# A PixArt-style block chain on one core: the cross attention's query pieces, key parts and rows of negated maxima go out by other DMA issues

## The reference, cut to what matters

```
q_c = q_c.reshape(B, N, NH, hd).transpose(0, 2, 1, 3)
k_c = k_c.reshape(B, S, NH, hd).transpose(0, 2, 1, 3)
v_c = v_c.reshape(B, S, NH, hd).transpose(0, 2, 1, 3)
c_attn_w = jax.nn.softmax(jnp.einsum('bhqd,bhsd->bhqs', q_c, k_c) * scale, axis=-1)
c_attn_out = jnp.einsum('bhqs,bhsd->bhqd', c_attn_w, v_c)
```

## Time and profile before

| | |
|---|---|
| median of 3 runs | 5570.83 us (5566.85 to 5578.4) |
| profiled execution, its own time | 5582.41 us |
| its span, first to last instruction | 5580.6 us |
| mean granted TensorE clock over the span | 0.864 of full speed |
| PE busy | 4790.3 us (86%) |
| DVE busy | 3913.3 us (70%) |
| ACT busy | 2961.3 us (53%) |
| POOL busy | 1466.4 us (26%) |
| first exp of the three cross attention phases starts at | 490.7, 2237.8 and 4411.5 us |
| last exp of the three starts at | 1709.0, 3351.5 and 5468.9 us |

### The profile page before, as it was taken

One profiled execution on the slowest core, in us unless ns is written; L12 is line 12 of the kernel. 1 busy time (PEld: TensorE's weight loads), 2 busy tenths in 40 slices (PEclk: granted clock), 3 DMA queues, 4 the chain that ended last, 5 costly groups with the idle time before them and its releaser, 6 DMA issues. The chain is left out here.

```text
span 5580.6 us, 168125 instructions
## 1 busy us (share of the span) xinstructions
PE 4790.3 (86%) x72434; PEld 3025.4 (54%) x72434; DVE 3913.3 (70%) x7814; ACT 2961.3 (53%) x4527; POOL 1466.4 (26%) x1189
## 2 busy tenths in 40 slices
PE   4858999999998585999999997888676799999998
PEld 2634555555554362666666663564364366656654
DVE  5547888888883553888888873465454688889893
ACT  2323666766655332666666663215423366666665
POOL 1013444434420103333333310000200334333320
PEclk6667999999988666999999988999766699999998
DMA  3325555555530334666666630550242565556640
GB/s 81 69 62 174 158 166 172 156 180 159 165 125 10 77 61 140 198 205 206 204 200 201 193 118 18 166 175 1 53 71 54 173 188 188 185 186 193 190 155 17
DMA packets 481664, 766.00 MB, mean 137 GB/s; under 512 B 144922, under 2 KB 381882, under 8 KB 468538
## 3 DMA queue, kind: packets, MB, share of 16 engines
q1 hardware_dynamic: 462394, 741.14, 44.5%
q10 hardware_dynamic: 18528, 14.11, 1.1%
HBM read 465.48 MB, written 287.75 MB: 135 GB/s over the span
## 5 line engine op out<-in xcount | busy, mean ns | idle before, releaser
L1349 DVE TENSOR_REDUCE maxima<-ps 100x1 f32<-100x482 f32 (+1 forms) x4608 | 2743.0, 650 | 580.3 <-PE ps L1169 566.5
L1296 ACT ACTIVATE probs<-ps 128x800 f32<-128x800 f32 (+1 forms) x2304 | 1805.6, 833 | 573.6 <-PE ps L1192 562.7
L1169 PE MATMUL ps<-kst,qst 48*100 48x482 bf16 (+1 forms) x4608 | 1392.6, 420 | 137.1 <-DMA qst<-cross_q_parts 54.9
L1401 POOL TENSOR_TENSOR kparts<-kf,zero 128x512 bf16<-128x512 f32 (+2 forms) x448 | 545.0, 1217 | 2044.2 <-ACT kf L1268 2004.1
L1209 PE MATMUL ps<-probs,vals 128*9 128x100 f32 x36864 | 1047.9, 256 | 1.0 <-ACT probs L1296 0.9
L1209 PEld LDWEIGHTS ps<-probs,vals 128*9 128x9 f32 x36864 | 757.5, 92 | 240.3 <-issue 198.8
L1169 PEld LDWEIGHTS ps<-kst,qst 48*100 48x100 bf16 x4608 | 443.8, 123 | 797.7 <-DVE maxima L1349 452.5
L1192 PE MATMUL ps<-qst,kst 51*128 51x100 bf16 x18432 | 803.8, 210 | 81.2 <-ACT probs L1296 60.6
L1192 PEld LDWEIGHTS ps<-qst,kst 51*128 51x128 bf16 x18432 | 614.4, 99 | 224.9 <-issue 86.4
L763 ACT ACTIVATE probs<-ps 100x800 f32<-100x800 f32 x192 | 159.7, 837 | 369.0 <-PE ps L711 368.6
L1146 PE MATMUL ps<-ctxT,perm_wk_L 128*128 128x512 f32 (+1 forms) x576 | 327.6, 656 | 31.9 <-DMA ctxT<-ctx_turned 17.1
(11 more groups left out here) (260 smaller groups left out, 4528.0 us busy)
## 6 DMA issues: line engine op xcount, KB each, us to landing
kst<-ctx_k_stack SPq DMA_DIRECT2D x96, 2888.0 KB
ctx_k_stack<-kparts SPq DMA_DIRECT2D x192, 541.5 KB
ctx_k_stack<-kparts SPq DMA_DIRECT2D x192, 361.0 KB
ctok<-in_ctx_dram SPq DMA_DIRECT2D x64, 704.0 KB
ctx_k_stack<-kparts SPq DMA_DIRECT2D x192, 180.5 KB
ctx_turned<-ctxT SPq DMA_DIRECT2D x32, 722.0 KB, 3.4
cT<-ctx_turned SPq DMA_DIRECT2D x32, 722.0 KB, 5.5
ctxT<-ctx_turned SPq DMA_DIRECT2D x32, 722.0 KB
```

The source lines that it names most:

```text
L1169: nc.tensor.matmul(ps[0:N, at:at + w], g.qst[s][row0:row0 + CROWS, j, :], g.kst[s][row0:row0 + CROWS, j, a:a + w], start=True, stop=True). ...
L1296: nc.scalar.activation(probs[kt % 2][hf][0:kts[kt], :].rearrange("p (k n) -> p k n", k=2), src, ACT.Exp).then_inc(exp_done, 1)
L1349: nc.vector.reduce_max(maxima[:, col:col + 1], ps[0:N, at:at + widths[c]], AX.X).then_inc(m_read, 1)
L1401: return nc.gpsimd.tensor_tensor(out, src, g.zero[0:src.shape[0], 0:1].to_broadcast(list(src.shape)), ALU.add)
```

## The change

- Query stack: with `SLOT_K` and `SLOT_Q` exchanged, the query parts stand in the slots in the order 0, 1, 2, 0, 1, 0. Neighbouring slots now hold neighbouring rows of the DRAM array, so six DMAs of 24, 16 and 8 rows fill it where twelve of 8 rows did.
- Key parts: the six slots now hold part 0 three times, part 1 twice, part 2 once. Two DMAs write each part, from a source that repeats it, and they wait only for the step of POOL that completed this part (`split`, then `parts_ready`).
- The sums of batch b - 1 are written to DRAM before the context load is issued and read back after it (`sp_out`, `sp_out_back`).
- The six rows of negated maxima are issued by ACT, three after exp 16 and three after exp 17 (`act_negmax`, `plan.turn() + 1` is 8 in all three plans). `sp_negmax` is gone.
- `dve_out` waits for the DMAs that read the same buffer three batches earlier.

```
-SLOT_K = (0, 1, 2, 0, 1, 0)
-SLOT_Q = (0, 0, 0, 1, 1, 2)
+SLOT_K = (0, 0, 0, 1, 1, 2)
+SLOT_Q = (0, 1, 2, 0, 1, 0)
...
-    K_RUNS = ((0, 3), (3, 2), (5, 1))
-    KW = 16 * 2 * len(K_RUNS)
-    Q_SLOTS = ((0, 3), (3, 2), (5, 1))
+    RUNS = ((0, 3), (3, 2), (5, 1))
+    KW = 16 * 2 * len(RUNS)
...
+        def act_negmax(k, e):
+            b, s, r = k.b, k.s, k.r
+            wait(g.act, neg_steps, 4 * b + 4)
+            for part in range(3):
+                at = HALF * e + CROWS + part
+                g.act.dma_start(g.qst[s][at:at + 1, :, :], nparts[8 * e:8 * e + 8, part, :]).then_inc(neg_loaded[s], 16)
+
         def act_slot(slot):
...
                 if k is not None:
                     act_exp(k, 2 * kt)
+                if kt == plan.turn() + 1 and k1 is not None:
+                    act_negmax(k1, 0)
...
                 if k is not None:
                     act_exp(k, 2 * kt + 1)
+                if kt == plan.turn() + 1 and k1 is not None:
+                    act_negmax(k1, 1)
...
         def dve_out(k):
             wait(g.dve, pv_done, KT * (k.b + 1))
+            wait(g.dve, o_moved[k.s], 96 * k.r)
...
             for e in range(2):
-                for part, (first, copies) in enumerate(Q_SLOTS):
-                    src = g.qx[b // per, e, part].rearrange("(d j) n -> d j n", j=PAIRS)[:, :, N * (b % per):N * (b % per) + N]
-                    for slot in range(first, first + copies):
-                        at = HALF * e + HD * slot
-                        sp.dma_start(g.qst[s][at:at + HD, :, :], src).then_inc(qst_loaded[s], 16)
-
-        def sp_negmax(k):
-            b, s, r = k.b, k.s, k.r
-            sp = g.sp
-            wait(sp, neg_steps, 4 * b + 4)
-            for e in range(2):
-                for part in range(3):
-                    at = HALF * e + CROWS + part
-                    sp.dma_start(g.qst[s][at:at + 1, :, :], nparts[8 * e:8 * e + 8, part, :]).then_inc(neg_loaded[s], 16)
+                rows = g.qx[b // per, e].rearrange("t (d j) n -> (t d) j n", j=PAIRS)
+                for first, n in RUNS:
+                    at = HALF * e + HD * first
+                    sp.dma_start(g.qst[s][at:at + HD * n, :, :],
+                                 rows[0:HD * n, :, N * (b % per):N * (b % per) + N]).then_inc(qst_loaded[s], 16)
...
-            wait(sp, parts_ready, len(CUTS) * (b + 1))
-            for first, n in K_RUNS:
+            for part, (first, n) in enumerate(RUNS):
+                if part < 2:
+                    wait(sp, split, 3 * (len(CUTS) * (b + 1) - 1) + (1, 3)[part])
+                else:
+                    wait(sp, parts_ready, len(CUTS) * (b + 1))
                 for e in range(2):
-                    sp.dma_start(slot_rows(s, e, first, n), parts[HALF * e:HALF * e + HALF, 0:n, :]).then_inc(k_written[s], 16)
+                    sp.dma_start(slot_rows(s, e, first, n),
+                                 parts[HALF * e:HALF * e + HALF, part:part + 1, :].to_broadcast([HALF, n, S])).then_inc(k_written[s], 16)
...
             if slot.k(2) is not None:
                 sp_stacks(slot.k(2))
+            if slot.k(-1) is not None:
+                sp_out(slot.k(-1))
             if slot.k(5) is not None:
                 sp_load_ctx(slot.k(5))
             if slot.k(-1) is not None:
-                sp_out(slot.k(-1))
+                sp_out_back(slot.k(-1))
             if context == "raw" and slot.k(3) is not None:
                 sp_keep_ctx(slot.k(3))
-            if slot.k(1) is not None:
-                sp_negmax(slot.k(1))
             if slot.k(3) is not None:
                 sp_keys_out(slot.k(3))
```

More of the change, by code:

```diff
@@ L980, in tiles, with turn @@
         return made
+    def turn(self):
+        return [kt for kt in range(len(self.scores)) if "turn" in [p[0] for p in self.early.get(kt, ()) + self.late.get(kt, ())]][0]
     def preps(self, kt):
@@ L1163, in pe_max @@
                 wait(g.pe, k_loaded[s], 16 * (r + 1))
-                wait(g.pe, qst_loaded[s], 16 * 12 * (r + 1))
+                wait(g.pe, qst_loaded[s], 16 * 2 * len(RUNS) * (r + 1))
             pe_ring_free(slot, x)
@@ L1296, in act_exp @@
             nc.scalar.activation(probs[kt % 2][hf][0:kts[kt], :].rearrange("p (k n) -> p k n", k=2), src, ACT.Exp).then_inc(exp_done, 1)
+        def act_negmax(k, e):
[4 more added lines that the diff above has]
+                g.act.dma_start(g.qst[s][at:at + 1, :, :], nparts[8 * e:8 * e + 8, part, :]).then_inc(neg_loaded[s], 16)
         def act_slot(slot):
-            k, k4 = slot.k(0), slot.k(4)
+            k, k1, k4 = slot.k(0), slot.k(1), slot.k(4)
             for kt in range(KT):
@@ L1496, in sp_out, with sp_out_back @@
             sp.dma_start(g.oscr[s], osb[s][:, :]).then_inc(o_moved[s], 16)
+        def sp_out_back(k):
+            b, s, r = k.b, k.s, k.r
+            sp = g.sp
             wait(sp, o_moved[s], 96 * r + 16)
@@ L1613, in _ @@
                 sp_out(known(B - 1).k(0))
+                sp_out_back(known(B - 1).k(0))
                 if context == "raw":
```

## The result

The changed kernel takes 6196 us (median of 4 runs, 6193 to 6226), the kernel before 5575 beside it: ratio 1.1125, 95% interval 1.1085 to 1.1165. It is slower by 622 us where 177 were predicted, and lies outside the range. The profiled execution has a span of 6196.7 us against 5580.6, and a mean granted clock of 0.807 against 0.864.

What follows compares the result with a forecast made beforehand. PE's own work was the floor in the second and third phase, with SP's late queue above it. Second +50, third +43, first +96, filling -12: +177 on 5571 gives 5748 us; own case 5643 to 5906, 8-in-10 range 5610 to 5930.

Steps and rivals of the forecast that it cites:

- SP bounds the second and third phase: SP's late queue keeps mean slots 1.4 and 1.8 us above PE's floor; relieving it brings at most 41 and 53 us.
- the floors of 33.8 and 32.0: Second- and third-phase slots in which nothing goes wrong, full of PE's own work at the full clock, in us.
- ACT absorbs: Rival: ACT takes the six issues without delay, so 106 us go away and the time is 5465; chance 0.11.
- Filling, -12: While each phase fills, six fewer query pieces bring PE's first maxima forward by 4.2 us, three times: -12 us.
- Four edits at nothing: Later read-back, key parts one by one, DVE's new wait and the parts' other order: nothing in a running slot.
- the first two: The later read-back and the key parts one by one, in SP's queue, said to cost nothing.
- six fewer give back 4.2: In SP's queue, six query pieces fewer, at 0.70 us each, shorten its round by 4.2 us.
- Six issues at 0.66 us: On ACT after exps 16 and 17, six row issues take 3.96 us; ends 0.59 and 0.72 each.
- The rival that said so: Rival: SP's key parts hold up two of ACT's six issues, 1.9 us a slot, 5913 us; chance 0.10.
- Passed on 1:1: Later exps lengthen each slot by the full delay: 3.3, 2.15 and 2.3 us in the three phases.
- The clock: PE's waits lower the clock in half the second- and third-phase slots: 1.0 us a slot; first phase none added.
- What the new profile would show: Signs: ACT issues near 0.6 us, PE waiting at kt 9 and 10, SP idle, slots near 42, 37 and 35 us.

Runs made afterwards that it cites:

- e1: The changed kernel with the six rows of negated maxima back on SP's queue, ahead of the key parts; 5487 us.
- e5: The changed kernel with one edit undone: SP waits for all three key parts before it issues the first; 5826 us.
- e3: The changed kernel, with SP waiting for the landing of the six rows before it issues the key parts; 5796 us.
- e10: The kernel before with only the two stacks' orders exchanged; rows on SP, sums written behind the context load as before; 5558 us.
- e11: The changed kernel with the rows back on SP and the key parts waiting for the last one; 5494 us.
- e2: The kernel before with only the six rows moved to ACT's queue, and DVE's wait for the read-back; 5822 us.
- e9: The changed kernel with key parts held until the rows land and ACT's six issues spread, one after each of exps 16 to 21; 5601 us.
- e6: The changed kernel, with SP issuing the first key part early (two transfers) and holding the other four until the rows have landed; 6133 us.
- e13: The changed kernel with each key part written once, six transfers of 180.5 KB, the other rows of the stack holding constants; 5854 us.
- e8: The changed kernel with the six rows issued by POOL, after it has split the keys; 5977 us.

## Why the prediction missed

**SP bounds the second and third phase: right.** With SP relieved and ACT left alone (e1) these phases stand at 33.99 and 32.04 us, at the floors of 33.8 and 32.0. The gain was put at 41 + 53 at most and is 1.22 x 29 + 1.79 x 29 = 87 us. The first phase did not move (38.75). The waits of the third phase without a releaser, read as a late stack, fell from 20.7 us to 1.8. What the rival "ACT absorbs" hoped for, 5465, is nearly what e1 reaches (5487), but with the rows on SP.

**Filling, -12: about right.** PE's first wait for the pieces falls from 25.6 to 22.5 us in the second phase and from 29.3 to 25.5 in the third (e1), 3.1 and 3.8 where 4.2 each were reckoned. What is left of the span of e1 beside 29 slots of each phase is 2439.2 us, and 2453.2 before: -14, but three more slots of each phase are in it.

**Four edits at nothing: the step that failed, twice.** Two of them are nothing: DVE's wait (no row of the changed kernel shows DVE waiting for a DMA there) and, with rows on SP, the key parts one by one. But *"the first two move issues inside a queue that now has some 9 us to spare, which is their cover"* looked at SP's queue alone. The key parts are up to 541.5 KB each, and leaving earlier put them under way just as ACT issues: 370 us (e5), 400 if they are held back behind the rows (e3). And the edit to the sums, put at nothing as a later read-back, carries most of the gain: 64 of 84 us (e10, e11). And *"six fewer give back 4.2"* was wrong by itself; it needs the sums written out ahead of the context load, so that they land while SP issues it.

**Six issues at 0.66 us: right alone, wrong in this kernel.** Alone 0.627 us (e2, e3, e5), in company 1.064 in the median and 6.67 us for six. The rival that said so had a chance of 0.10, and *"Nothing in the rows shows one queue holding the other"* looked too narrowly: the trace of before shows what matters, on one queue. The key parts' line there, and two single issues behind the first two:

```profile
L1489 SPq DMA_DIRECT2D ctx_k_stack<-kparts x576: 580/1342/2723, 415.1 to 5395.2; - x192
...
2518.55 2.09 SPq L1489 DMA_DIRECT2D ctx_k_stack<-kparts  x1
2520.69 2.40 SPq L1489 DMA_DIRECT2D ctx_k_stack<-kparts  x1
```

The third and fourth key part take 2.09 and 2.40 us to issue where the shortest take 0.58: an issue waits when much is under way. The question should have been what is under way when ACT issues, and the order of the lists with POOL's times gave the answer. I priced that rival at 5913, two issues at 1.588 us, 1.9 us a slot. The issues came to 6.67 - 3.82 = 2.85 us a slot more than in e3, and a slot to 2.2, 5.8 and 5.0 us more in the three phases: in the second and third the clock doubled it (against the windows of e3 idle time grew by 2.9 and 2.4 us a slot, the matmuls by 3.0 and 2.6).

**Passed on 1:1: right in size.** In e3, the kernel without the collision, exp 18 starts 4.36 us after exp 16, 2.33 later than before (2.15 predicted), and the mean slots are 42.15, 37.78 and 35.49 where 42.1, 36.95 and 35.3 were predicted. Its 5796 us lie 48 over the forecast and inside its range. But the reason given, that any later exp moves all that follows, is not the whole of it: spread out, the same six issues cost the second phase nothing (e9). PE can be two halves of scores ahead of ACT. In the second and third phase three issues in a block outlast that (PE waits 57 and 60 us for ACT in e3), one does not (0.6 and 0.4 in e9).

**The clock: mis-sized.** +1.0 us a slot in the second and third phase, none in the first. By windows over e3 like those above, the same matmuls take 29.4 us longer in the second phase (1031.47 against 1002.05), 19.5 in the third (950.45 against 930.94), so 1.0 and 0.7 a slot, but 62.0 in the first (1118.48 against 1056.47), 2.1 a slot, where none was added. There the slot came out right for a partly wrong reason: of the 3.35 us that it grew by only 1.2 are waiting. In the changed kernel, with gaps of 2 to 3 us, it is 2.2, 4.0 and 3.2 us a slot.

**What the new profile would show.** PE's waits for ACT at kt 9 and 10, no wait for the rows but three, SP idle: all there. Issues of 0.6 us, slots near 42, 37 and 35: not; they are the profile of e3.

## What to carry to other kernels

An issue is not a fixed price: before moving one to a compute engine's list, look at what is under way at that moment, and read the longest issues of large transfers on any queue as the sign of how much is too much. A transfer that is sent earlier is not free because its queue has time; ask whose issue it will stand in front of. And if a compute engine must issue, put single issues between its instructions rather than a block: in the second and third phase here the engine that it feeds then hardly waited for it, and the whole kernel was 195 us faster (e9 against e3).

## What the runs showed of the hardware that was not expected

- ACT's issue of a 1.6 KB transfer took 0.627 us alone, and 1.49 and 2.35 us with two transfers of 541.5 KB sent ahead and SP's queue silent (e6); with 180.5 KB for each of the six transfers it took 0.627 in the median (e13).
- POOL's issue of the same transfer was not held up (0.518 us, at most 0.702), but the data landed a median 4.0 us after it (e8).
- With six pieces between a load of 2888 KB and the context, the issue of the context's second piece, 18 KB, took 3.17 to 4.86 us in the second phase (e10); with twelve pieces between them it took 0.50 to 2.01 (before).
- Around two gaps of PE of 2.04 and 3.20 us, within 7 us, the granted clock fell, after the first of them, and stood at 0.50 for the 9.5 us behind the second; in three windows of 29 slots the same matmuls took 275 us longer than before.
